# Where GpSimd scatters the routed tokens' slots inside the attention steps of a fused transformer layer, and when the slot table is fetched

## The reference, cut to what matters

```python
xn  = _layernorm(x)
out = x + attn(xn) + ffn(xn)

# attn: per batch b and head h (32 pairs), t = 1024
S = jnp.einsum('bhqd,bhkd->bhqk', Q, K) * scale
S = jnp.where(causal, S, NEG)
P = jax.nn.softmax(S, axis=-1)
O = jnp.einsum('bhqk,bhkd->bhqd', P, V)

# ffn: the router picks 2 experts of 8 for each token, with weights
topk_idx, topk_w = _route(x2d, router_weight, bias)
out = sum over e of cw[:, e] * mlp_e(x2d)  +  mlp_shared(x2d)
```

## Time and profile before

| | us |
|---|---|
| median of 3 runs (1099.39 to 1101.45) | 1099.41 |
| the profiled execution's own time | 1100.83 |
| its span | 1099.1 |
| TensorE busy | 1015.2 (92% of the span) |
| VectorE busy | 725.8 (66%) |
| ScalarE busy | 635.4 (58%) |
| GpSimd busy | 514.3 (47%) |

### The profile page before, as it was taken

The page is one execution under the profiler, slowest core; times in us unless marked ns, Lnnn a source line. Parts: engine busy times, 40 slices in busy tenths (PEclk is TensorE's granted clock), DMA queues, the critical chain, the costliest instruction groups (busy, mean ns, idle before and its releaser), DMA issues. The chain is left out here.

```text
span 1099.1 us, 18059 instructions
## 1 busy us (share of the span) xinstructions
PE 1015.2 (92%) x5059; PEld 792.7 (72%) x5060; DVE 725.8 (66%) x1451; ACT 635.4 (58%) x1278; POOL 514.3 (47%) x568
## 2 busy tenths in 40 slices
PE   5999979987799998999999999978789999999994
PEld 4867867765577876777777777757677787777882
DVE  6732333654477777887778777644378888888872
ACT  3323211265588888888788878862165655555550
POOL 0012823488766656676676765650013433333321
PEclk9999989988899999999999999989889999999998
DMA  6988997352564664666547565248698533444322
GB/s 202 343 334 339 178 271 251 135 114 49 128 181 103 180 182 145 159 146 178 162 103 195 149 193 146 55 139 273 207 330 240 92 69 70 77 76 75 69 51 36
DMA packets 125863, 176.58 MB, mean 161 GB/s; under 512 B 61680, under 2 KB 80368, under 8 KB 122192
## 3 DMA queue, kind: packets, MB, share of 16 engines
q1 hardware_dynamic: 115440, 154.81, 48.7%
q0 software_dynamic: 9760, 20.49, 9.8%
q10 hardware_dynamic: 576, 0.26, 0.1%
HBM read 105.57 MB, written 61.55 MB: 152 GB/s over the span
## 5 line engine op out<-in xcount | busy, mean ns | idle before, releaser
L1339 POOL TENSOR_TENSOR prob_lo<-prob,prob_hi 128x512 fp32r<-128x512 f32 (+2 forms) x320 | 318.4, 1011 | 169.9 <-ACT prob_hi L1384 131.2
L1377 ACT ACTIVATE prob<-ps_s 128x512 f32<-128x512 f32 (+3 forms) x384 | 188.0, 490 | 107.7 <-PE ps_s L1591 65.8
L1384 ACT ACTIVATE prob_hi<-prob 128x512 fp32r<-128x512 f32 (+3 forms) x384 | 198.8, 518 | 12.5 <-ACT row_stage L1358 12.1
L1457 DVE CUSTOM_DVE_ANT_0 ps_m<-ps_m,causal 128x384 f32<-128x384 f32 (+3 forms) x256 | 126.1, 497 | 79.8 <-PE ps_m L1562 75.5
L1956 DVE TENSOR_TENSOR rw_lo<-gu_sb,rw_hi 128x704 fp32r<-128x704 f32 x156 | 138.9, 892 | 51.2 <-ACT rw_hi L1900 45.6
L1900 ACT ACTIVATE rw_hi<-gu_sb 128x704 fp32r x156 | 123.6, 794 | 60.5 <-PE ps_ru L1989 43.3
L1586 PE MATMUL ps_s<-qs,ks 97*128 97x512 f32 (+3 forms) x384 | 138.5, 361 | 12.2 <-ACT prob L1377 10.4
L1873 POOL DMA_INDIRECT out<-work,slot_table x39 | 62.8, 1610 | 182.3 <-DVE work L1941 152.9
L1609 PE MATMUL ps_o<-prob_hi,vs 128*66 128x512 f32 (+3 forms) x384 | 132.2, 344 | 13.1 <-issue 10.9
L1562 PE MATMUL ps_m<-ks,qs 96*128 96x512 f32 (+3 forms) x384 | 132.2, 344 | 2.4 <-DVE maxima L1457 2.4
L1611 PE MATMUL ps_o<-prob_lo,vs 128*66 128x512 f32 (+3 forms) x384 | 130.9, 341 | 0.0
(11 more groups left out here) (194 smaller groups left out, 2205.9 us busy)
## 6 DMA issues: line engine op xcount, KB each, us to landing
xt<-xt_blocks SPq DMA_DIRECT2D x7, 2048.0 KB
v_rows<-work SPq DMA_DIRECT2D x16, 512.0 KB, 3.0
xt_blocks<-xt SPq DMA_DIRECT2D x4, 2048.0 KB, 11.1
qk_hi<-work SPq DMA_DIRECT2D x8, 1024.0 KB, 4.6
qk_lo<-work SPq DMA_DIRECT2D x8, 1024.0 KB, 7.3
qs<-qk_hi SPq DMA_DIRECT2D x64, 128.0 KB, 2.9
ks<-qk_hi SPq DMA_DIRECT2D x64, 128.0 KB, 3.2
vs<-v_rows SPq DMA_DIRECT2D x32, 256.0 KB, 3.0
```

Source lines behind the costliest of these rows:

```text
L1339: nc.gpsimd.tensor_tensor(prob_lo[:, s % NPL, 0:w], prob[:, s % NP, 0:w], prob_hi[:, s % NPH, 0:w].bitcast(F32), ALU.subtract).then_inc(lo ...
L1377: nc.scalar.activation(prob[:, s % NP, 0:w], ps_s[s % NS][:, 0:w], ACT.Exp, scale=SCALE).then_inc(exp_done, 1)
L1384: nc.scalar.activation(prob_hi[:, s % NPH, 0:w], prob[:, s % NP, 0:w], ACT.Copy).then_inc(hi_ready, 1)
L1457: nc.vector.tensor_tensor_reduce(ps_m[s % NM][:, 0:w], ps_m[s % NM][:, 0:w], causal[:, TBW - w:], 1.0, MASKED, ALU.add, ALU.max, maxima[:, ...
```

## The change

Two things are changed. The pieces of `place` that are left when the steps begin are no longer put behind every step, but behind steps n of a head in `PLACE_BEHIND`: those whose remainder VectorE computes (4 and 8) and those whose block is 256 columns wide or narrower (1, 3, 5, 9). These are six of twelve. The condition `BLOCKS[n][1] >= 4 * BLOCKS[n][0] + 2` picks the key tiles that are cut by two tiles or more. And the table is read back at step 360 instead of step 192.

```diff
     LO_DVE = [4, 8]
     LO_POOL = [n for n in range(NB) if n not in LO_DVE]
 
+    PLACE_BEHIND = [n for n in range(NB) if n in LO_DVE or BLOCKS[n][1] >= 4 * BLOCKS[n][0] + 2]
+
@@
-    TABLE_AT = STEPS // 2
+    TABLE_AT = STEPS - 2 * NB
@@
                                                 prob_hi[:, s % NPH, 0:w].bitcast(F32),
                                                 ALU.subtract).then_inc(lo_pool, 1)
-                    next(placing_steps, None)
+                    if n in PLACE_BEHIND:
+                        next(placing_steps, None)
```

## The result

| | before | after |
|---|---|---|
| median, us | 1099.99 (1099.39 to 1101.45, 4 runs) | 1088.07 (1086.93 to 1093.97, 4 runs) |
| profiled execution's own time | 1100.83 | 1088.62 |
| its span | 1099.1 | 1086.9 |

The ratio after to before is 0.9905, 95% interval 0.9877 to 0.9933. The two medians alone give 0.9892, inside that interval. The kernel became faster by 0.95%, where 1.44% was forecast: the direction and the place were right, the measured gain was a third smaller than the forecast one. The median lies just outside the forecast's own range (1080 to 1088 us) and inside its range for 8 in 10.

What follows compares the result with a forecast made beforehand. GpSimd was taken to bound the heads with scatters, costing 28.3 us; spreading them leaves a 12.5 us loss, so 15.8 us are won: 1099.41 - 15.8 = 1083.6 us, own range 1080 to 1088, 8 in 10 1079.5 to 1089.5.

Steps and rivals of the forecast that it cites:

- What bounds, and the size of the loss before: Four heads with scatters: GpSimd sets the pace, 88.20 us against 59.92 at TensorE's pace, so placement costs 28.3 us.
- One bound of the forecast: Changed stretch: with scatters at 0.98 + 0.17 = 1.15 us each, the loss is 9.1 us.
- The price of GpSimd's work: A head with six scatters: 9.8 us of remainders + 6 x 1.254 = 17.3 us on GpSimd, against TensorE's 14.98.
- rival 1: Same 5.3 heads: GpSimd's work swells beside a busier VectorE, loss 36.7 us, time 1107.8; chance 4%.
- From there to the remainder of step 73, GpSimd works without a break: From step 9's remainder at 228.8 us: 92.2 us of unbroken GpSimd work, so step 73 starts at 321.0.
- small holes: GpSimd gaps before wide blocks in the changed stretch, taken to cancel against TensorE's reserve of about a step.
- The loss forecast: Changed stretch to step 73: 12.3 us behind TensorE's pace plus 0.2 for gaps between remainders, 12.5 us.
- rival 4: Heads with scatters: TensorE is late for something else, such as ScalarE's copy of `ps_o`; time stays at 1099; chance 2%.
- I expect no fall: Changed stretch: TensorE has 14.98 us of work in 17.3, 87%, so its granted clock stays at 1.00.
- rival 2: Heads with scatters: clock falls in the longer stretch, no longer hidden, 3 to 8 us more, 1087 to 1092; chance 10%.
- The table: Fetch moved from step 192 to 360: gain 0 at the old place, cost 0 at the new, bounds -0.5 and +1.
- free pace: Attention heads without scatters: TensorE sets the pace, 14.98 us a head or 1.248 us a step.

Runs made afterwards that it cites:

- table: The kernel before with only the slot table's fetch moved, to step 360 from 192: 1099.57 us, ratio 0.9993.
- before_one: The kernel before, with VectorE's 128x4 maximum reading one tensor instead of two: 1099.50 us, ratio 0.9996.
- cut: The changed kernel plus a GpSimd memset of 128x1 and a wait for it behind step 11 of each head: 1083.37 us, ratio 0.9835.
- wide: The changed kernel with its pieces behind the other six steps (0, 2, 6, 7, 10, 11), the wide blocks: 1093.37 us, ratio 0.9944.

## Why the prediction was right in its sum and wrong in its result

**What bounds, and the size of the loss before: right.** The 28.3 us over four heads were there again in table and before_one (148.5 to 149.3 us for eight heads), and with three places all but 2.7 us of it went from these heads. One bound of the forecast is added up wrongly: with scatters at 1.15 us its loss is 9.3, not 9.1; nothing hangs on it.

**The price of GpSimd's work: right.** 17.3 us a head was forecast. The two heads of after in which TensorE waited for VectorE 0.5 us or less took 16.8 and 17.2 (though VectorE operations of 3.01 and 2.52 us stand in them), and the five in cut took 17.2 to 17.5. ScalarE's exp waited 6.4 us for remainders on GpSimd, against 22.8. A scatter cost as much as before: 30 of them were busy for 31.84 us, 1.06 each, against 1.04. So rival 1, scatters that swell beside a busier VectorE, didn't happen.

**"From there to the remainder of step 73, GpSimd works without a break": this step failed.** So did the one that let TensorE's reserve cancel "small holes". GpSimd had 8.2 us of holes. They were made by itself: it shut VectorE out for 4.2 to 4.8 us three times, VectorE held TensorE, TensorE ran on at half clock, and then GpSimd had no input. In before a scatter, with 0.17 us ahead of it, stood between any two remainders and VectorE came through there. The change took this gap away at the one place where four remainders, three of them 512 wide, stand together. The loss forecast was 12.5 us; in the eight heads it was 138.7 - 119.8 = 18.9, and 12.2 in cut, where only the run is broken. The missing 6.4 to 6.7 us are this one thing with the falls of the clock behind it, shown by taking it away: the second to fourth heads took 60.4 us in after and 52.0 in cut, and the other five together 1.6 us more in cut, about what eight breaks of 0.18 us cost. No rival of the prediction had it. The nearest was rival 4 (TensorE late for something else, 2%), which named the copy of `ps_o` and a time of 1099.

I had looked at the lock of the shared port in one direction alone, VectorE holding up GpSimd's scatters. The Trainium skill, "SBUF — State Buffer", section "SBUF: two separate sides", names the other as well: a VectorE instruction with two inputs in SBUF against a GpSimd instruction that reads SBUF, the later one waiting in full. The trace agrees: at most 0.17 us with one input, up to 4.83 or 5.25 with two. Which of two came first can't be read off the start times: the three maxima began 0.35 to 0.47 us ahead of the first wide remainder, beside a scatter, and waited nonetheless. That a queue of GpSimd instructions can keep the port from one to the next is what the runs here add.

**"I expect no fall" of the clock: wrong, by the same cause.** The granted clock was 0.84, 0.91 and 0.91 in the three heads with a shut-out and 1.00 in the next two. With the run cut it was 0.99 over the whole stretch. So these falls followed TensorE's waits for VectorE (3.26, 2.25 and 2.47 us), and weren't an effect of the longer stretch alone, as rival 2 had it. Such a fall isn't bound to VectorE: in wide the clock fell behind waits of 2.02 and 2.29 us at the first value matmul of a head (but not behind four others of 1.9 to 2.3), and in cut once, soon after TensorE had stood for 1.08 us. What decides whether it falls is not shown.

**The table: right, nothing.** Ratio 0.9993, and 365.1 us from step 96 to the last remainder with either place.

**The whole.** The profiled executions differ by 12.2 us: 9.7 in the eight heads, 2.2 ahead of them (in before the clock fell once more, at 183 us), and 0.3 behind. The forecast had 15.8, all in the heads. Even the 2.2 us by which after was lucky ahead of the steps does not make up for what was lost.

## What to carry to other kernels

Before you pack an engine's queue tighter, look at what used the gaps. Where GpSimd and VectorE both read SBUF, a run of GpSimd instructions that are all ready can be one long block for a VectorE instruction with two SBUF inputs, however small, so look for the smallest operations of VectorE on TensorE's way and what GpSimd runs beside them. And work that is too much for an engine is better spread until the engine is no longer the bound (three or four pieces in a head, ratios 0.9813 and 0.9802) than until it is only a little late (six, 0.9905).

## What was not expected of the hardware

- GpSimd instructions that are ready in its queue can keep a two-input VectorE instruction out from one to the next: four of them in 4.45 us held a 128x4 maximum for 4.83 us. A memset of 0.10 us with a wait for itself was gap enough. At 249.72 and 269.25 us VectorE came in ahead of the last of the four, with no gap on GpSimd to be seen; why there is open.
- At the free pace the same remainders start just as closely, and the maximum takes 0.75 to 1.17 us, about one of them. There a remainder starts about 0.1 to 0.2 us after its `prob_hi` is there (in after, at 336.79 and 338.03 us), where those of the run at 228.70 had been ready for 0.5 to 1.3 us. That the later input is what lets VectorE in fits, but was not tested.
- The change of one input tensor moved the stall to the next instruction with two inputs, on the same engine, which then took 5.25 us instead of 0.68.
